# Attention heads on one core: another order of the head rounds, and a second buffer for the second half of the rank rows

## What is computed

```
draft  = q @ k.T                          # rotated q and k, future keys at -3.4e38
keep   = the 128 largest entries of each draft row (top_k)
scores = draft / 4, all that is not kept or lies in the future at -3.4e38
out    = softmax(scores) @ v
```

## Time and profile before

| | before |
|---|---|
| time, median of 3 runs | 3250.77 us (3249.15 to 3252.75) |
| time of the profiled execution | 3250.62 us |
| its span | 3248.7 us |
| TensorE, VectorE, ScalarE, GpSimd busy, share of the span | 90%, 76%, 61%, 51% |
| the heads | from about 2065 us to about 3125 us of the span |
| TensorE, VectorE, ScalarE, GpSimd busy in the 278.7 us from 2249.3 | 224.85, 229.89, 253.27, 194.94 us |

### The profile page before, as it was taken

One profiled execution on the slowest core, in us unless ns is written; L12 is line 12 of the kernel. 1 busy time (PEld: TensorE's weight loads), 2 busy tenths in 40 slices (PEclk: granted clock), 3 DMA queues, 4 the chain that ended last, 5 costly groups with the idle time before them and its releaser, 6 DMA issues. The chain is left out here.

```text
span 3248.7 us, 50391 instructions
## 1 busy us (share of the span) xinstructions
PE 2916.7 (90%) x15823; PEld 1785.8 (55%) x15929; DVE 2466.6 (76%) x4628; ACT 1982.2 (61%) x4218; POOL 1650.4 (51%) x3659
## 2 busy tenths in 40 slices
PE   8999999999999999999999998567888878888879
PEld 4455455454554554554645545346666666666654
DVE  5677697696796876976967877578888888888746
ACT  2464564564554545545645433599999999899723
POOL 3235254263362452542633655677676767677503
PEclk9999999999999999999999999668889898888879
DMA  2222132232231222322321210000000000000010
GB/s 93 59 81 94 66 104 72 75 120 79 72 107 69 88 88 72 104 76 76 112 76 61 89 35 27 1 1 2 2 2 1 2 1 2 2 1 2 2 50 27
DMA packets 65803, 169.62 MB, mean 52 GB/s; under 512 B 11776, under 2 KB 19328, under 8 KB 64512
## 3 DMA queue, kind: packets, MB, share of 16 engines
q1 hardware_dynamic: 54448, 115.17, 10.9%
q10 hardware_dynamic: 11088, 51.19, 4.5%
HBM read 161.08 MB, written 5.24 MB: 51 GB/s over the span
## 5 line engine op out<-in xcount | busy, mean ns | idle before, releaser
L2052 ACT ACTIVATE X<-ah_z,ah_trial 128x256 bf16<-128x256 f32 (+6 forms) x896 | 732.0, 822 | 25.1 <-POOL ah_trial L2155 14.1
L1207 ACT ACTIVATE m_mix<-m_mix,m_cs 128x128 f32<-128x128 f32 x1024 | 312.9, 388 | 255.5 <-DMA m_mix<-cs_rows 255.3
L2007 PE MATMUL ah_ps_o<-a_v,X 128*128 128x17 f32 x2304 | 353.0, 281 | 0.3 <-DVE hT L2252 0.3
L2007 PEld LDWEIGHTS ah_ps_o<-a_v,X 128*128 128x128 f32 x2304 | 339.0, 221 | 0.6 <-issue 0.6
L1089 POOL TENSOR_TENSOR m_xdec<-m_xdt,m_decay_out 128x512 f32<-128x512 f32 x112 | 142.0, 1267 | 213.7 <-DVE m_xdt L1333 202.1
L1117 POOL TENSOR_TENSOR m_squares<-m_squares 128x256 f32<-128x256 f32 x128 | 107.3, 839 | 273.4 <-ACT m_squares L1219 273.4
L2063 ACT ACTIVATE X<-ah_ps_e 128x512 f32<-128x512 f32 (+3 forms) x384 | 184.4, 481 | 94.2 <-PE ah_ps_e L1994 61.4
L1013 PE MATMUL m_ps_x<-m_w_out,m_gate 128*128 128x512 f32 x512 | 233.7, 599 | 0.0
L1013 PE MATMUL m_ps_d<-m_w_out,m_gate 128*128 128x512 f32 x512 | 233.5, 599 | 0.0
L2237 DVE MAX8 ah_top<-ah_ps_m 128x8 f32<-128x256 f32 (+6 forms) x224 | 185.5, 828 | 38.4 <-PE ah_ps_m L1957 34.8
L2224 DVE TENSOR_SCALAR_CACHE_REDUCE X<-ah_z,ah_cut 128x256 bf16<-128x256 f32 (+6 forms) x224 | 193.4, 874 | 22.9 <-POOL ah_cut L2160 22.9
(11 more groups left out here) (319 smaller groups left out, 7578.1 us busy)
## 6 DMA issues: line engine op xcount, KB each, us to landing
m_mix<-cs_rows SPq DMA_DIRECT2D x128, 512.0 KB, 4.4
m_w_proj<-in_w_proj ACTq DMA_DIRECT2D x69, 512.0 KB, 3.3
m_fade<-fade_rows SPq DMA_DIRECT2D x224, 128.0 KB, 2.9
m_w_out<-in_w_out ACTq DMA_DIRECT2D x7, 2048.0 KB, 7.8
X<-in_x SPq DMA_DIRECT2D x8, 256.0 KB, 5.0
m_w_out<-in_w_out SPq DMA_DIRECT2D x1, 2048.0 KB, 10.0
x_away<-X SPq DMA_DIRECT2D x1, 2048.0 KB, 7.3
X<-x_away SPq DMA_DIRECT2D x8, 256.0 KB, 6.2
```

What stands on the lines that cost most here:

```text
L1207: act.activation(mix[:, u % 3, h, :], mix[:, u % 3, h, :], ACT.Relu, bias=cs[:, c, h0 + h:h0 + h + 1], scale=-1.0).then_inc(lag_done, 1)
L2007: last = pe.matmul(ps_o[:, t, :], eT[:, g % 3, b * P:(b + 1) * P], v[:, b0 + b, h // REP, :], start=i == 0 and b == 0, stop=b0 + b == t, s ...
L2052: act.activation(sign[:, at % 2, 0:(t + 1) * P], z[:, h % RING, cols(t)], ACT.Sign, bias=trial[:, h % RING, 0, t - 1:t], scale=-1.0, accum ...
```

## The change

On TensorE chunk 0 of head n-3 moves to the front of the round, ahead of `scores(n+1, 0)`; chunk 1 alone stays behind `sample`; chunk 2 moves behind `scores(n+1, 1)`, where chunk 3 is. The second half of the rows is turned at t=5 and no longer at t=7. On VectorE the takes of tiles 1 and 2 go ahead of `divide(n-4)`. The buffer `rows` gets a third part: the second half now alternates between two parts by the head's parity, so that its copy waits for chunk 11 of head h-2 and no longer of head h-1. ScalarE makes that copy at slot 24 and no longer after slot 27.

```diff
-    CHUNKS_FIRST = (0, 1, 2)
+    CHUNK_AHEAD = (0,)
+    CHUNKS_FIRST = (1,)
     CHUNKS_AFTER_MARKED = ((), (), (), (), (), (7,), (9,), ())
-    CHUNKS_AFTER_SCORES = ((), (3,), (4,), (5,), (6,), (8,), (10,), (11,))
+    CHUNKS_AFTER_SCORES = ((), (2, 3), (4,), (5,), (6,), (8,), (10,), (11,))
...
-    ROWS_BEFORE = {14: 0, len(SWEEPS) * W: 1}
+    ROWS_BEFORE = {14: 0, 24: 1}
...
-        rows = sb("rows", [P, S], BF16)
+        rows = sb("rows", [P, 3, BANK], BF16)
...
+        rows_at = lambda h, half: half * (1 + h % 2)
...
             for n in range(FIRST, LAST):
+                if live(n - 3):
+                    turn_and_add(n - 3, CHUNK_AHEAD)
                 if live(n + 1):
                     scores(n + 1, 0)
                     sample(n + 1)
...
-                    if live(n - 2) and t in (2, 7):
-                        turned_rows(n - 2, t // 7)
+                    if live(n - 2) and t in (2, 5):
+                        turned_rows(n - 2, t // 5)
...
                 act.wait_ge(row_done, 2 * h + half + 1)
-                if h:
-                    act.wait_ge(et_done, (h - 1) * NCH + LAST_CHUNK[3 if half == 0 else 7] + 1)
-                act.activation(rows[:, half * BANK:(half + 1) * BANK], ps_x[:], ACT.Copy).then_inc(rows_done, 1)
+                if half == 0 and h:
+                    act.wait_ge(et_done, (h - 1) * NCH + LAST_CHUNK[3] + 1)
+                elif half and h >= 2:
+                    act.wait_ge(et_done, (h - 2) * NCH + LAST_CHUNK[7] + 1)
+                act.activation(rows[:, rows_at(h, half)], ps_x[:], ACT.Copy).then_inc(rows_done, 1)
...
-                if live(n - 2):
-                    row_out(n - 2, ROWS_BEFORE[at])
...
-                if live(n - 4):
-                    divide(n - 4)
                 if live(n - 2):
                     take(n - 2, 1)
                     take(n - 2, 2)
+                if live(n - 4):
+                    divide(n - 4)
```

More of the change, by code:

```diff
@@ L1987, in exponents @@
                                   skip_group_check=True)
-                pe.matmul(out[:, 0:w, :], minus_rows[:], rows[:, t * P:(t + 1) * P].unsqueeze(1).to_broadcast([P, w, P]),
+                pe.matmul(out[:, 0:w, :], minus_rows[:], rows[:, rows_at(h, t // 4), t % 4 * P:(t % 4 + 1) * P].unsqueeze(1).to_broadcast([P, w, P]),
                           start=t == 0, stop=False, skip_group_check=True)
```

## The result

| | before | after |
|---|---|---|
| median | 3252.75 us (3249.07 to 3256.96, 7 runs) | 3240.47 us (3238.41 to 3242.47, 7 runs) |
| profiled execution | 3250.62 us, span 3248.7 | 3242.47 us, span 3240.6 |
| 27 full rounds, cut to cut | 844.79 us, 31.29 each | 831.79 us, 30.81 each |

The ratio is 0.9958, with a 95% interval of 0.9948 to 0.9969. The change made the kernel faster by 0.4%, some 12 us, where I had forecast 48. The time lies above my range.

What follows compares the result with a forecast made beforehand. No engine is full, so a chain through VectorE's last copy, TensorE's round start, divide, takes and picks sets the round. Rounds falling from 31.29 to 29.5 us over 27 rounds gain 48: 3250.6 less 48 is 3202 us, range 3184 to 3229.

Steps and rivals of the forecast that it cites:

- Which clock: TensorE's round start: two gaps of about 0.9 us, low clock in 4 rounds of 10, mean round 29.5 us.
- rival 2: TensorE's clock falls in every round: rounds of 30.5 us, a gain of 21, 3229 us; chance 0.18.
- second case below: The skill's rule on TensorE's clock, taken strictly, was said to lead here: clock falling every round, 30.5 us each.
- rival 1: TensorE's clock stays high in all rounds: 28.83 us each, a gain of 66, 3184 us; chance 0.20.
- two prices: Round time by TensorE's clock: 28.83 us at the high level, 30.5 us at the low one.
- w: VectorE's new wait for marked scores of tile 2: 0 at high clock, 1.8 us taken at low.
- chain at the low clock: Last count, cut, take, VectorE's picks, chunk 7, next last count: 28.7 us plus VectorE's new wait, 30.5 us together.
- ScalarE's own work: ScalarE's busy time in a round, put at 28.1 us.
- rival 3: No change within 0.2%: something unseen, such as ScalarE's waits for exponents, sets rounds of 31.05 to 31.5 us; chance 0.05.
- Fill and drain: Rounds where the pipeline fills or drains: costed at nothing, a us each way.
- GpSimd loop: GpSimd's queue from last counts to slot 14, 14.77 us, plus ScalarE's other half, 14.06: a 28.83 us round.
- slot's 0.5 us: ScalarE's second copy at slot 24 costs 0.5 us a round in GpSimd's loop; floor without it 28.3 us.

Runs made afterwards that it cites:

- e1: The changed kernel with five unread 512-column matmuls added in each of TensorE's two idle gaps at the round's start; ratio 0.982, median 3195.49 us.
- e8: The changed kernel with only the first gap, ahead of the scores, filled with five matmuls; ratio 0.9892.
- e9: The changed kernel with only the second gap, ahead of the first take's mark, filled with five matmuls; ratio 0.9934.
- e4: The kernel before with one edit, the takes of tiles 1 and 2 ahead of the divide; ratio 1.0018.
- e2: The changed kernel with chunk 2 put back ahead of the marked scores of tile 1; ratio 0.996 against the kernel before.
- e5_before_fill: The kernel before with eight unread matmuls added in TensorE's 2.0 us gap ahead of the scores of tile 0; ratio 0.9876, median 3209.74 us.

## Why the prediction was wrong

- **The step that failed** is the one headed "Which clock": "I take the low clock in 4 rounds of 10". It was low at the start of every full round, 8 us a round by the mean clock. I had reasoned that gaps of 1 us in mid-round leave it high, and that two near each other lie between those and 2.00. The trace of after and the runs e1, e8 and e9 show that these two cost the clock every time, one alone in part of the rounds. The premise was too simple as well: in e1_fill the clock fell in a gap of 1.09 us in mid-round. The prediction's own sign of being wrong, a round start at the low clock as often as before, is what came: 27 rounds of 27 in both kernels. The low clock was one of the two cases that I had priced, so rival 2 (0.18) came, and a little worse.
- **The inference from the Trainium skill** (TensorE: Matmul & The Clock Gate, "What's actually happening") was wrong too: "Taken strictly, its rule leads to the second case below". Taken as the prediction gives it, that a gap that is mostly filled should leave the clock high, the rule leads to rival 1, the clock high in all rounds, and no round of the changed kernel bore that out.
- **The two prices were right.** High clock: 28.83 worked out, 28.83 or 28.84 in 15 of 27 rounds of e1_fill, though with luck in the parts: in its round 12 they are 14.63 and 14.20, not 14.77 and 14.06. Low clock: 30.5 worked out, 30.76 in round 9 and 30.81 on average; w was 1.8, and 1.82 us are in the trace. From 29.5 to 30.81 in 27 rounds are 35 of the 40 us missed on the profiled execution.
- **The chain at the low clock** ran as worked out, through VectorE's picks and chunk 7. In round 9 it is 4.83 us from the end of the last count (2333.59) to the cut, 0.24 to the take, 14.12 to the end of the pick of tile 4 (2352.78; worked out 12.07 + 1.8 = 13.87), 1.52 to chunk 7 and 10.04 to the end of the next last count (2364.34; worked out 10.05). So the difference to 30.5, 0.25 us a round, lies on VectorE between the take and that pick. ScalarE's waits for chunks 2 and 4 lie beside this chain: it waits another 0.81 us for chunk 7, which comes 1.52 us behind the pick as before.
- **ScalarE's own work** I had too small, 28.1 us a round for 28.5. With 2.7 us of waits a round before the change and 2.3 after (73.8 and 62.7 us over the 27 rounds) work and waits fill the round in both kernels. And its waits for exponents did what rival 3 feared: they didn't go with VectorE's wait, they grew, from 55.4 to 62.7 us. Of the 80.4 us that VectorE no longer waits ahead of the reciprocal, 11 us reached ScalarE, the engine with the least idle time.
- **Fill and drain** I had costed at nothing. Round 3 took 33.90 us (31.07 before), rounds 31 and 32 took 29.88 and 31.62 (28.88 and 29.36): 6 us more. They move in every run with clock and order, and I can't say which part is whose.
- **The GpSimd loop, the wait of the takes for the cut, the divide's wait gone, no new wait at slot 24:** as forecast. The slot's 0.5 us was shown at the high clock. That ScalarE's own work ends at the same 28.3 us as that loop without the copy, the prediction didn't see.
- **The takes ahead of the divide** I had called a gain by itself. Alone they gain nothing (e4, 1.0018), since the marked scores of tile 1 still stand behind chunk 2. And with chunk 0 ahead of the scores and chunk 2 at its old place (e2) TensorE waits for the divide, through the product of chunk 0. The prediction saw neither; in the changed kernel chunk 2's new place avoids both.

## What to carry to other kernels

Where TensorE waits in short gaps, read the granted clock next to each gap before a reordering is priced: two gaps of 1.2 us cost as much of the clock here as one of 2.0 (8.0 and 7.5 us at the low level a round), and the clock alone (1.2% in e5_before_fill) was worth more than the whole change (0.4%). A few filling matmuls in the gap, whose result nobody reads, show at once what the clock is worth; look whether they end before the engine could have gone on, as they did here by 0.32 us. Then look for the engine that has no idle time left: ScalarE's 28.3 us end every gain by order here. When an instruction is moved back on one engine, list who waits for its result and what stands behind that: in e2_chunk2 the divide, moved behind two takes, stopped TensorE for 1.4 us a round through a product that I hadn't had in view.

## What the runs showed of the hardware

In round 9 of the changed kernel TensorE had gaps of 1.19 and 1.25 us with 1.7 us of work between them. Its eight products between the gaps still took 1.02 us, as at the high level, and from the second gap on it was at 1.2 GHz, at least for the 6 us of the three windows above (2339 to 2345), in two of which it was never idle. All 27 full rounds have such a fall. Once both gaps were filled, the mean clock rose from 0.87 to 0.97. A fall in mid-round stayed in 14 of the 27 rounds of e1_fill, in round 9 in a gap of 1.09 us. The Trainium skill (TensorE: Matmul & The Clock Gate, "HAM oscillation — how this bites in real kernels") puts the fall down to a long wait between bursts; here the longest of TensorE's waits at a round's start were 2.3 us before and 1.9 after, most of them 2.0 and 1.2, and both traces have the fall. What that page of the Trainium skill says of a second kind ("A second HAM failure mode: psum-queue depth-cycling"), an engine that idles for short times and often, is nearer to these rows.
